# First jobs of a layer-1 attention between the tiles of the down projection, in buffers of their own

## The chip, the core and the metric

The kernel runs on one core of one Trainium2 chip. Its time is the device time of one launch in microseconds (us). The core's engines work side by side and wait for each other only through semaphores: PE (TensorE, matmuls and transposes into PSUM), DVE (VectorE), ACT (ScalarE), POOL (GpSimd), and SP, which issues most of the loads.

## The reference

Two decoder layers over x of 4 x 256 tokens and 256 channels. Each layer adds to x an attention, a state-space model (SSM) with a gate, and a feed-forward part. The stretch that is changed is the end of layer 0's feed-forward part, layer 1's attention, and beside both the steps of layer 1's SSM, which depend on the context alone:

```python
x = x + _L0_ffn_ref(_layernorm(x), ...)      # hdn = silu(g) * u ; out = hdn @ down_w
x = x + _L1_attn_ref(_layernorm(x), ...)     # 16 heads, 4 key heads, D = 128, causal
x = x + _L1_xattn_ref(ctx_1024, _layernorm(x), ...)

qkv = x @ w_qkv                              # q, k: layernorm over D, then rotary
q = q * cos + _rotate_half(q) * sin
weights = softmax(q k^T / sqrt(D), causal)
attn = weights @ v ; out = attn @ w_o

def step(state, xs):                         # the SSM: a scan over 256 tokens,
    dA = exp(d_t[..., None] * A)             # for 16 states of 256 channels
    state = state * dA + (d_t * u_t)[..., None] * B_t
    y_t = einsum('ben,bn->be', state, C_t)
```

## The kernel before

All engines run hand-written programs; the order on each is the order of the code, and every engine is in order. Tokens lie on partitions in 8 tiles of 128 (two per batch element b = 0 to 3).

**Feed-forward of layer 0.** The up projection runs over 12 half tiles j (PE L1631, ACT L730, DVE L1216 and L1219). The down projection (PE L1651, function `fd`) makes 8 output tiles of 12 matmuls each into PSUM banks 4 and 5 (tokens of b = 0, 1, "half 0") and 2 and 3 (half 1). DVE then adds a half to x (`fd_residual`, L1053), takes its layernorm statistics (L1024, L1028), POOL makes the reciprocal root (L393, L394), DVE applies it (`ln_apply`, L1033), PE transposes the half (`ln_tr`, L1474), and ACT and DVE copy it to hT (L622, L1039).

**Quarter steps.** Layer 1's SSM has 64 of them (4 batch elements x 16 states). A step q is: ACT, two exponentials into dA (L605); DVE, the product (`dbq`, L997) and the scan (`scanq`, L1006); POOL, the product with C (L403); PE, 4 transposes that accumulate (`accq`, L1435). The buffers form a ring of 8. The first `Q_IN_FFN` steps stand in code of the feed-forward part, the others in the attention's plan.

**Attention 1.** Per batch element there is a job for the keys (i = 0), four for the queries (i = 1 to 4), each for 512 columns, and one for the values. A job (b, i): PE projects (L1671, 8 matmul passes); ACT squares (`sq`, L757); DVE multiplies with the rotary tables (`rot`, L1257, L1261), sums the squares (`sum`, L1269); POOL makes the reciprocal root (L459, L460); DVE adds and scales (`rope`, L1274, 8 x L1280); PE transposes (`tr`, L1708) and ACT copies (`trc`, L768). The tables come from `tables()` (L1203 to L1207, 10 DVE instructions). A unit u = 0 to 63 is one head of one b: PE the scores (`s`, L1718 the mask by a matmul with the identity, L1719, L1720), DVE two maxima (`max`, L1288, L1289), ACT two exponentials (`exp`, L782, L784), DVE the division (`norm`, L1294, L1296, L1297), PE three transposes (`pt`, L1729), ACT a copy (`ptc`, L791), PE the values (`pv`, L1738, L1739), ACT a copy (`at`, L797), PE the output projection (`o`, L1750).

**What sets the order.** The function `att1_plan` writes one list, `ATT1_PLAN`; each engine walks it and takes its own kinds. In slot u stand, in this order, `s` of u + 1, a job's `tr`, `norm` of u - 1, `pv` of u - 2, `max` and `exp` of u, `o` of u - 3, `proj` and `acc`, `da`, `sq`, `pt` of u - 1, then `rope`, `rot`, `sum` and the quarter steps. Jobs are put in by hand at slots relative to units; the quarter steps are dealt out by `att1_plan` from the costs of the jobs and PE's load. `bank_order` says which PE work has to have left banks 0 and 1 before a projection or a transpose may write there (`BEFORE`). ACT takes the square of job j only when DVE has summed job j - 1 (L755).

Of the kernel before, what the change touches and what calls it, by code (L numbers as in the profile page):

```python
# [2061 lines left out]
```

## Time and profile before

| | us |
|---|---|
| three runs, median | 913.36 (910.98 to 916.4) |
| the profiled execution | 913.75 |
| its span | 912.0 |
| DVE busy | 703.3 (77%) |
| PE busy | 767.7 (84%) |
| ACT busy, POOL busy | 445.6 (49%), 340.6 (37%) |

The span runs from the first to the last instruction of the profile; the profiled execution is 1.75 us longer than it. The share of an engine is over all stages. Attention 1 lies between about 334 and 674 us of the span.

### The profile page before, as it was taken

What the parts mean: (1) busy time and instruction counts of PE and PEld (TensorE: products, weight loads), DVE (VectorE), ACT (ScalarE), POOL (GpSimd) and SP (SyncE); (2) the same over time, 40 slices, a digit from 0 to 9 for tenths busy, and PEclk for the clock granted to TensorE, in tenths of its full rate; (3) what the DMA queues carried; (4) which work ended last, traced back from release to release, by engine and by line L of the source; (5) the groups of instructions that cost most, each with busy time, mean ns of one, the idle gap of its engine ahead of it and who ended that gap; (6) DMA issues with size and microseconds to landing.
All of it is one profiled execution on the core that took longest, in us unless ns stands there. A gap on an engine that the chain in (4) does not pass through costs nothing.

```text
span 912.0 us, 12288 instructions
## 1 busy us (share of the span) xinstructions
PE 767.7 (84%) x3984; PEld 563.1 (62%) x3984; DVE 703.3 (77%) x1229; ACT 445.6 (49%) x928; POOL 340.6 (37%) x242
## 2 busy tenths in 40 slices
PE   6771459877798996799999999999955799999997
PEld 2241346554433563477767776777743689999996
DVE  4869779889857976999999999999977544444443
ACT  1663368650336402666566556756642354444442
POOL 1001346552330422233333323432343286666663
PEclk9785579998799998999999999999987899999999
DMA  4313223345020212011111211111300243334431
GB/s 171 121 47 114 93 94 125 115 139 218 1 98 0 74 43 92 19 40 44 51 36 36 69 36 36 55 39 36 118 0 1 79 158 138 138 138 138 141 135 46
DMA packets 28884, 74.63 MB, mean 82 GB/s; under 512 B 3633, under 2 KB 6337, under 8 KB 28449
## 3 DMA queue, kind: packets, MB, share of 16 engines
q1 hardware_dynamic: 28384, 71.51, 23.2%
q10 hardware_dynamic: 448, 2.49, 0.8%
q8 instruction: 25, 0.41, 0.2%
q14 instruction: 27, 0.21, 0.1%
HBM read 72.55 MB, written 1.44 MB: 81 GB/s over the span
## 4 chain that ended last, share of the span: by engine, by line
PE 50%; DVE 26%; issue 11%; ACT 9%; POOL 3%; DMA 1%; POOLq 0%; DVEq 0%; SPq 0%; ACTq 0%
PE ps L1671 6%; PE ps L1785 6%; PE ps L1786 6%; PE ps L1787 6%; PE ps L1631 4%; DVE hS L976 3%; PE ps L1651 3%; PE ps L1750 3%; PE ps L1435 2%; PE ps L1738 2%; DVE arena L1280 2%; DVE hS L1006 2%; DVE ps L968 2%; PE ps L1408 1%; PE ps L1720 1%
## 5 line engine op out<-in xcount | busy, mean ns | idle before, releaser
L403 POOL TENSOR_TENSOR hS<-hS,BCb 128x512 f32<-128x512 f32 x64 | 81.6, 1278 | 131.9 <-issue 66.7
L1387 DVE SCALAR_TENSOR_TENSOR arena<-ps,arena 128x1024 f32<-128x1024 f32 x32 | 39.2, 1224 | 102.2 <-ACT arena L842 93.1
L426 POOL TENSOR_TENSOR hS<-hS,BCb 128x1024 f32<-128x1024 f32 x23 | 56.1, 2440 | 111.3 <-DVE ps L968 96.3
L1671 PE MATMUL ps<-WB,hT 128*128 128x512 f32 x192 | 88.0, 603 | 3.0 <-DVE arena L1261 2.0
L476 POOL TENSOR_TENSOR MHl<-arena,MHh 128x1024 fp32r<-128x1024 f32 x34 | 81.7, 2404 | 16.9 <-ACT MHh L845 16.9
L1416 PE MATMUL ps<-ident,hS 128*128 128x128 f32 x256 | 40.1, 311 | 54.7 <-POOL hS L426 31.2
L1785 PE MATMUL ps<-Wh,MHh 128*128 128x256 f32 x272 | 77.8, 286 | 6.0 <-POOL MHl L476 6.0
L1006 DVE TENSOR_TENSOR_SCAN hS<-dA,ps 128x512 f32<-128x512 f32 x64 | 78.1, 1220 | 2.2
L1786 PE MATMUL ps<-Wl,MHh 128*128 128x256 f32 x272 | 77.6, 285 | 0.0
L1787 PE MATMUL ps<-Wh,MHl 128*128 128x256 f32 x272 | 77.5, 285 | 0.0
L1416 PEld LDWEIGHTS ps<-ident,hS 128*128 128x128 f32 x256 | 32.6, 159 | 65.1 <-POOL hS L426 38.2
L473 POOL TENSOR_TENSOR Wl<-WB,Wh 128x512 fp32r<-128x512 f32 x34 | 47.3, 1392 | 64.2 <-ACT Wh L826 64.2
L1750 PE MATMUL ps<-WA,arena 128*128 128x256 f32 x256 | 65.7, 380 | 0.0
L1671 PEld LDWEIGHTS ps<-WB,hT 128*128 128x128 f32 x192 | 36.9, 194 | 40.6 <-issue 38.4
L976 DVE TENSOR_TENSOR_SCAN hS<-dA,ps 128x1024 f32<-128x1024 f32 x23 | 52.6, 2286 | 8.2 <-ACT dA L591 7.5
L1785 PEld LDWEIGHTS ps<-Wh,MHh 128*128 128x128 f32 x272 | 52.7, 194 | 8.3 <-POOL MHl L476 7.1
L605 ACT ACTIVATE dA<-DEL,negA 128x255 f32<-128x255 f32 x128 | 55.4, 504 | 0.0
L1785 PE MATMUL ps<-hTh,Wh 128*128 128x512 f32 x136 | 53.8, 396 | 0.0
L1786 PE MATMUL ps<-hTl,Wh 128*128 128x512 f32 x136 | 53.5, 394 | 0.0
L1786 PEld LDWEIGHTS ps<-Wl,MHh 128*128 128x128 f32 x272 | 52.8, 194 | 1.2
L1787 PE MATMUL ps<-hTh,Wl 128*128 128x512 f32 x136 | 53.1, 390 | 0.0
L1787 PEld LDWEIGHTS ps<-Wh,MHl 128*128 128x128 f32 x272 | 52.7, 194 | 0.0
(233 smaller groups left out, 1967.4 us busy)
## 6 DMA issues: line engine op xcount, KB each, us to landing
BCb<-bc_dram SPq DMA_DIRECT2D x32, 512.0 KB, 3.7
BCb<-bcq_dram SPq DMA_DIRECT2D x64, 256.0 KB, 3.1
arena<-gate_dram SPq DMA_DIRECT2D x32, 512.0 KB, 3.7
WB<-in_we SPq DMA_DIRECT2D x34, 256.0 KB, 2.7
WB<-in_wqkv SPq DMA_DIRECT2D x1, 3072.0 KB, 12.7
WA<-in_wo ACTq DMA_DIRECT2D x1, 2048.0 KB, 7.7
WA<-in_ffn SPq DMA_DIRECT2D x1, 1408.0 KB, 7.9
pkb<-in_pk SPq DMA_DIRECT2D x2, 698.0 KB, 4.7
```

The costliest lines, as they stand in the source:

```text
L403: gp.tensor_tensor(h, h, qbc(q)[:, 1:2, :].broadcast_to([P, DT, S]), ALU.mult).then_inc(s["c_ready"], 1)
L426: gp.tensor_tensor(h, h, BCb[g % SB_LOADS][:, 1:2, :].broadcast_to([P, DT, HALF]), ALU.mult).then_inc(s["c_ready"], 1)
L476: gp.tensor_tensor(MHl[:, p, :], MH[p], MHh[:, p, :].bitcast(F32), ALU.subtract).then_inc(s["m_lo"], 1)
L605: sc.activation(qring(dA, q)[:, d, 1:S], DEL[:, d, S * b + 1:S * b + S], ACT.Exp, scale=negA[:, d * DS + n:d * DS + n + 1]).then_inc(s["da ...
L976: v.tensor_tensor_scan(f(h), f(a), f(dbu(g)), 0.0, ALU.mult, ALU.add).then_inc(s["scan_done"], 1)
L1006: v.tensor_tensor_scan(f(qring(hS, q)), f(qring(dA, q)), ps[:, DBQ_BANK, :], 0.0, ALU.mult, ALU.add).then_inc(s["scan_done"], 1)
L1416: last = mm(ps[:, ACC_BANK + j // 2, 256 * (j % 2) + P * d:256 * (j % 2) + P * d + P], src[:, d, P * j:P * j + P], ident[:], start=(first ...
L1671: last = mm(ps[:, bank + t, :], hT[:, c, P * (2 * b + t):P * (2 * b + t) + P], WB[:, c, c0:c0 + 512], start=(c == 0), stop=(c == HC - 1))
L1750: last = mm(ps[:, 5, 256 * t:256 * t + 256], aT1[u % 2][:, P * t:P * t + P], WO1[:, h, :], start=(h == 0 and t == 0), stop=(h == H1 - 1), ...
L1785: mm(out, wh, xh, start=start, stop=False, **kw)
L1786: mm(out, wh, xl, start=False, stop=False, **kw)
L1787: return mm(out, wl, xh, start=False, stop=stop, **kw)
```

## The change

- `Q_IN_FFN` goes from 10 to 14, so steps 10 to 13 stand ahead of the attention's plan.
- `tables()` moves from behind the first half's layernorm into the up projection, behind half tile 3.
- The down projection's tiles 4, 5 come first, then the transposes of half 0, tile 6, the projections of jobs 0 and 1, and only then tile 7 and the transposes of the quarter steps.
- Jobs 0 and 1 get buffers of their own (free arena, pkb, H, ctxp), job 1 banks 4 and 5, the values of b = 0 banks 2 and 3.
- The residual of half 1 stands between the two jobs' `rot` and `sum`; its statistics go to slot 4, its `ln_apply` to slot 6, its transposes to slot 11.
- Jobs (0, 2), (0, 3), (0, 4) go to slots -1, 2 and 4 (they were at -3, 0 and 3).
- The mask matmul writes 256 columns in place of 384.

```diff
-Q_IN_FFN = 10
-Q_GROUP_ENDS = (1, 3, 7, 9, QSTEPS - 1)
+Q_IN_FFN = 14
+Q_GROUP_ENDS = (1, 7, 8, 9, 13, QSTEPS - 1)
...
-        job_bank = lambda j: 2 if j == 1 else 0
...
-        v_bank = lambda b: 0 if b else 4
+        tok2 = lambda a: a.rearrange("p (t n) -> p t n", t=2)
+        JA_FIRST = [tok2(ar(24, 1024)), tok2(pkb[:, 0:1024])]
+        JB_FIRST = [tok2(ar(28, 1024)), tok2(H[:, 0:4, :].rearrange("p a b -> p (a b)"))]
+        JS_FIRST = [tok2(ar(36, 1024)), tok2(ctxp.rearrange("p b s -> p (b s)")[:, 0:1024])]
+
+        job_bank = lambda j: 4 if j == 1 else 0
...
+        v_bank = lambda b: 0 if b else 2
...
+                if j == 3:
+                    tables()
...
-            quarters(step, 2)
+            quarters(step, 1)
             ln_apply(3, 0)
-            tables()
-            fd_residual(1)
-            ln_stats(3, 1)
+            quarters(step, 1)
             ln_tr_copy(2, 0)
-            ln_apply(3, 1)
+            quarters(step, 4)
...
-            fd(0)
+            fd(0, 1, 2, 3)
             for k in range(4):
                 accq(next(step))
-            fd(1)
-            for q in step:
-                accq(q)
+            fd(4, 5)
             ln_tr(2, (0,))
+            fd(6)
...
-                mm(ps[:, 2 + p, 0:3 * P], identb[:], mask1[:], start=True, stop=True, skip_group_check=True)
+                diagonal = lambda z: z.rearrange("p (k n) -> p k n", k=3)[:, 0::2, :]
+                mm(diagonal(ps[:, 2 + p, 0:3 * P]), identb[:], diagonal(mask1[:]), start=True, stop=True, skip_group_check=True)
...
-    rope_job(-8, 0, 0, 2, 3)
-    rope_job(-7, 0, 1, 2, 3)
-    at(-7, "wo1", 0)
-    at(-6, "ln1", 0)
-    v_job(-5, 0)
+    first, second = (0, 0), (0, 1)
+    both = lambda j: [(kind, j + (x,)) for x in range(2) for kind in ("tr", "trc")]
+    ramp = [("proj", first), ("sq", first), ("proj", second), ("sq", second), ("fd7", 0),
+            ("rot", first), ("sum", first), ("rot", second), ("fd1", 0), ("sum", second),
+            ("v", 0), ("vc", 0), ("wo1", 0), ("rope", first)] + both(first) + [("rope", second)] + both(second)
+    rope_job(-1, 0, 2, 2, 3)
+    rope_job(2, 0, 3, 2, 4)
+    rope_job(4, 0, 4)
+    at(4, "stats1", 0)
+    at(6, "apply1", 0)
+    at(11, "ln1", 0)
...
-    plan = []
+    plan = ramp
```

PE from the first four tiles of the down projection to the first scores, before (L1651 the down projection, L1474 the layernorm's transposes, L1671 projections, L1708 a job's transposes, L1718 to L1720 scores):

```order
L1651 MATMUL ps<-arena 128x256 x24
L1435 MATMUL ps<-ident,hS 128x128 x16
L1651 MATMUL ps<-arena 128x256 x24
L1435 MATMUL ps<-ident,hS 128x128 x16
L1474 MATMUL ps<-ident,H 128x128 x8
L1671 MATMUL ps<-WB,hT 128x512 x8
L1474 MATMUL ps<-ident,H 128x128 x8
L1708 MATMUL ps<-ident,arena 128x128 x8
L1671 MATMUL ps<-WB,hT 128x512 x4
L1708 MATMUL ps<-ident,arena 128x128 x8
L1671 MATMUL ps<-WB,hT 128x512 x4
L1718 MATMUL ps<-mask,identb 128x384
```

The same place of the changed kernel (L1663, L1486, L1682, L1719 and L1732 are the same functions):

```order
L1663 MATMUL ps<-arena 128x256 x24
L1447 MATMUL ps<-ident,hS 128x128 x16
L1663 MATMUL ps<-arena 128x256 x12
L1486 MATMUL ps<-ident,H 128x128 x8
L1663 MATMUL ps<-arena 128x256 x6
L1682 MATMUL ps<-WB,hT 128x512 x8
L1663 MATMUL ps<-arena 128x256 x6
L1447 MATMUL ps<-ident,hS 128x128 x32
L1682 MATMUL ps<-WB,hT 128x512 x4
L1719 MATMUL ps<-ident,arena 128x128 x8
L1719 MATMUL ps<-ident,pkb 128x128 x8
L1732 MATMUL ps<-mask,identb 128x2x128
```

The two projections now stand ahead of the last down-projection tile, and the third job's projection, which stood ahead of the first scores, stands behind them. Half 1's transposes have left this place.

DVE of the changed kernel from the second job's `sum` (L1275) to the first steps of the plan, slots 0 to 2 (L1280 and L1286 `rope`, L1294 and L1295 `max`, L1263 and L1267 `rot`, L1300 `norm`, L1003 and L1012 a step):

```order
L1275 TENSOR_REDUCE jst<-ctxp 128x8
L1280 TENSOR_TENSOR arena<-arena 128x1024
L1286 SCALAR_TENSOR_TENSOR arena<-arena,jst,tabs 128x128 x8
L1280 TENSOR_TENSOR pkb<-pkb,H 128x1024
L1286 SCALAR_TENSOR_TENSOR pkb<-pkb,jst,tabs 128x128 x8
L1294 TENSOR_REDUCE nm<-ps 128x1
L1295 TENSOR_REDUCE nm<-ps 128x1
L1263 TENSOR_TENSOR arena<-ps,tabs 128x1024
L1267 TENSOR_TENSOR arena<-ps,tabs 128x8x64 x2
L1275 TENSOR_REDUCE jst<-arena 128x8
L1300 RECIPROCAL rc<-sum 128x2
```

Before, DVE's rows at that place, from the third job's `rot` on:

```order
L1257 TENSOR_TENSOR arena<-ps,tabs 128x1024
L1261 TENSOR_TENSOR arena<-ps,tabs 128x8x64 x2
L1269 TENSOR_REDUCE jst<-arena 128x8
L1288 TENSOR_REDUCE nm<-ps 128x1
L1289 TENSOR_REDUCE nm<-ps 128x1
L1274 TENSOR_TENSOR arena<-arena 128x1024
L1280 SCALAR_TENSOR_TENSOR arena<-arena,jst,tabs 128x128 x8
L997 TENSOR_TENSOR ps<-DU,BCb 128x512
L1006 SCALAR_TENSOR_TENSOR hS<-dA,ps 128x512
L1294 RECIPROCAL rc<-sum 128x2
```

The third job's `rot` and `sum` stood ahead of the first `max` and a quarter step ahead of the first `norm`; now they stand between that `max` and `norm`, and no step.

ACT of the changed kernel in slots 0 to 2 (L774 `trc`, L763 `sq`, L788 and L790 `exp`, L797 `ptc`, L803 `at`, L611 the exponentials of steps 14 to 18):

```order
L774 COPY arena<-ps 128x512 x4
L763 ACTIVATE arena<-ps 128x1024
L788 ACTIVATE arena,sum<-ps,nm 128x128
L790 ACTIVATE arena,sum<-ps,nm 128x256
L788 ACTIVATE arena,sum<-ps,nm 128x128
L790 ACTIVATE arena,sum<-ps,nm 128x256
L797 COPY arena<-ps 128x384
L774 COPY arena<-ps 128x512 x2
L803 COPY arena<-ps 128x256
L788 ACTIVATE arena,sum<-ps,nm 128x128
L790 ACTIVATE arena,sum<-ps,nm 128x256
L611 ACTIVATE dA<-DEL,negA 128x255 x10
```

Before, the ten exponentials stood behind the first `exp`; now they stand behind the third. The dealt-out steps per slot, from 0 to 16, were 1 0 1 1 0 1 1 0 1 1 0 1 1 3 0 1 1 and are 0 0 2 0 0 0 3 0 0 0 0 1 1 3 0 0 1; slot 47 had one and has none, and otherwise the slots from 17 to 52 hold the same as before. Slots 7 to 10 hold `rope` of (0, 4) with `rot` and `sum` of (1, 0); nothing; `proj` of (1, 1) with `rope` of (1, 0); `rot` and `sum` of (1, 1).

## Rows read from the trace of the kernel before

**Rows 1.** Windows: busy us and count of PE, PEld, DVE, ACT, POOL; PEclk; DMA.

```profile
334.00:378.00 44.00, 30.17 (x99) 17.01 (x99) 31.99 (x68) 15.42 (x34) 9.35 (x10) 0.88 0.13 48
378.00:668.00 290.00, 278.66 (x1487) 209.28 (x1488) 281.64 (x632) 177.42 (x526) 98.83 (x87) 1.00 0.16 48
```

**Rows 2.** DVE in time: start, us, line, tiles, count, idle before with its releaser.

```profile
276.70 0.69 DVE L1216 SCALAR_TENSOR_TENSOR arena<-arena,ps 128x512 f32<-128x512 f32 x1 [7.48 <-ACT arena L730]
...
320.41 0.67 DVE L997 TENSOR_TENSOR ps<-DU,BCb 128x512 f32<-128x512 f32 x1
...
324.31 2.31 DVE L1033 TENSOR_SCALAR H<-X,lnmv,lnrs 128x256 f32<-128x256 f32 x4
...
326.54 0.41 DVE L1203 TENSOR_TENSOR tabs<-arena 128x256 f32<-128x256 f32 x1
...
329.80 0.42 DVE L1207 TENSOR_TENSOR tabs<-tabs,arena 128x256 f32<-128x256 f32 x1
...
331.25 1.22 DVE L1053 TENSOR_TENSOR X<-X,ps 128x1024 f32<-128x1024 f32 x1 [1.03 <-PE ps L1651]
...
335.66 1.39 DVE L1033 TENSOR_SCALAR H<-X,lnmv,lnrs 128x256 f32<-128x256 f32 x4 [0.90 <-POOL lnrs L394]
...
361.82 1.22 DVE L1257 TENSOR_TENSOR arena<-ps,tabs 128x1024 f32<-128x1024 f32 x1 [5.68 <-ACT arena L757]
...
365.28 0.28 DVE L1288 TENSOR_REDUCE nm<-ps 128x1 f32<-128x128 f32 x1
```

**Rows 3.** PE in order of time, down projection and attention.

```profile
319.25 11.89 PE L1651 MATMUL ps<-arena 128*128 128x256 f32 x48
...
357.12 3.60 PE L1671 MATMUL ps<-WB,hT 128*128 128x512 f32 x8
...
372.22 0.55 PE L1729 MATMUL ps<-ident,arena 128*128 128x128 f32 x3 [3.35 <-DVE arena L1297]
...
390.03 1.04 PE L1708 MATMUL ps<-ident,arena 128*128 128x128 f32 x8
...
403.25 0.33 PE L1718 MATMUL ps<-mask,identb 128*128 128x384 bf16 x1
...
406.46 0.49 PE L1729 MATMUL ps<-ident,arena 128*128 128x128 f32 x3
```

**Rows 4.** Windows of 2 us, for the granted clock (PEclk).

```profile
374.00:376.00 2.00, 2.00 (x9) 1.66 (x9) 2.00 (x3) 0.01 (x1) 0.00 (x0) 0.50 0.00 0
...
378.00:380.00 2.00, 1.46 (x8) 0.91 (x8) 1.97 (x5) 2.00 (x8) 1.53 (x2) 1.00 0.00 0
```

**Rows 5.** DVE in order of time, units 6 to 9 and the norm of unit 12.

```profile
399.67 0.14 DVE L1294 RECIPROCAL rc<-sum 128x2 f32<-128x2 f32 x1
...
400.84 1.21 DVE L1257 TENSOR_TENSOR arena<-ps,tabs 128x1024 f32<-128x1024 f32 x1
...
404.29 0.15 DVE L1294 RECIPROCAL rc<-sum 128x2 f32<-128x2 f32 x1
...
408.56 1.21 DVE L1274 TENSOR_TENSOR arena<-arena 128x1024 f32<-128x1024 f32 x1
...
411.91 0.69 DVE L997 TENSOR_TENSOR ps<-DU,BCb 128x512 f32<-128x512 f32 x1
...
413.77 0.14 DVE L1294 RECIPROCAL rc<-sum 128x2 f32<-128x2 f32 x1
...
427.88 0.14 DVE L1294 RECIPROCAL rc<-sum 128x2 f32<-128x2 f32 x1
```

**Rows 6.** DVE in order of time, near the attention's end.

```profile
644.61 0.17 DVE L1294 RECIPROCAL rc<-sum 128x2 f32<-128x2 f32 x1 [1.00 <-ACT arena L784]
```

**Rows 7.** ACT in order of time, attention 1.

```profile
366.73 4.08 ACT L605 ACTIVATE dA<-DEL,negA 128x255 f32<-128x255 f32 x10
...
390.67 1.08 ACT L768 COPY arena<-ps 128x512 f32<-128x512 f32 x2 [0.78 <-PE ps L1708]
```

**Rows 8.** POOL in order of time, up projection.

```profile
264.35 8.88 POOL L445 TENSOR_TENSOR WB<-WB,wmean 128x2560 f32<-128x2560 f32 x2 [16.73 <-DVE wmean L1194]
```

More of the change, by code:

```diff
@@ L289, in build @@
         TR_LNS = [0, 2, 3, 5]
-        TR_BANK = [(4, 6), (0, 2), (0, 4), (0, 2)]
+        TR_BANK = [(4, 6), (0, 2), (0, 0), (0, 2)]
         CONV_BANK = [0, 4]
@@ L452, in _ @@
                 times_cq(q)
-            ln_rstd(3, (1,))
             def job(j):
@@ L464, in _ @@
                     job(JOB[a])
+                elif kind == "stats1":
+                    ln_rstd(3, (1,))
                 elif kind == "dbu" and a > Q_IN_FFN:
@@ L1301, in _ @@
                     job(*a)
+                elif kind == "fd1":
+                    fd_residual(1)
+                elif kind == "stats1":
+                    ln_stats(3, 1)
+                elif kind == "apply1":
+                    ln_apply(3, 1)
                 elif kind == "ln1":
@@ L1645, in _, with fd @@
             pe.wait_ge(s["wdn_ready"], NI)
-            def fd(hf):
-                for t in range(4 * hf, 4 * hf + 4):
+            def fd(*tiles):
+                for t in tiles:
                     for i in range(NI):
                         m = mlen(i)
-                        last = mm(ps[:, FD_BANK[hf] + (t % 4) // 2, 256 * (t % 2):256 * (t % 2) + 256], hid0[0:m, i, P * t:P * t + P], WDN[0:m, i, :],
+                        last = mm(ps[:, FD_BANK[t // 4] + (t % 4) // 2, 256 * (t % 2):256 * (t % 2) + 256], hid0[0:m, i, P * t:P * t + P], WDN[0:m, i, :],
                                   start=(i == 0), stop=(i == NI - 1))
@@ L1684, in banks_free @@
                     pe.wait_ge(s["job_tr_copied"], 2 * JOB[b[:2]] + 2)
+                elif was == "ln1":
+                    ln_ready(2, 1)
                 else:
@@ L1689, in v_job @@
                 if b == 0:
-                    ln_ready(2, 1)
+                    pe.wait_ge(s["x_new"], XN_FFN)
                 banks_free("v", b)
@@ L1714, in s1 @@
                 pe.wait_ge(s["job_tr_copied"], 2 * max(JOB[b, 0], JOB[b, 1 + g]) + 2)
+                if u == 0:
+                    pe.wait_ge(s["v_copied"], 1)
                 if u >= 2:
@@ L1756, in _ @@
                     v_job(a)
+                elif kind == "fd7":
+                    fd(7)
+                    for q in step:
+                        accq(q)
                 elif kind == "ln1":
+                    banks_free("ln1", 0)
                     ln_tr(2, (1,))
@@ L1892, in v_job @@
         at(slot, "vc", b)
-    rope_job(-8, 0, 0, 2, 3)
-    rope_job(-7, 0, 1, 2, 3)
-    at(-7, "wo1", 0)
-    at(-6, "ln1", 0)
-    v_job(-5, 0)
+    first, second = (0, 0), (0, 1)
[9 more added lines that the diff above has]
+    at(11, "ln1", 0)
     for b in range(B):
         u = H1 * b
-        rope_job(u - 3, b, 2)
-        rope_job(u, b, 3)
-        rope_job(u + 3, b, 4)
+        if b:
+            rope_job(u - 3, b, 2)
+            rope_job(u, b, 3)
+            rope_job(u + 3, b, 4)
         if b + 1 < B:
@@ L1950, in att1_plan @@
             plan += [("pt", u - 1), ("ptc", u - 1)]
-        plan += pick("wo1", "rope", "rot", "sum")
+        plan += pick("rope", "rot", "sum", "stats1", "apply1")
         for kind, m in now:
@@ L1969, in bank_order @@
 def bank_order():
-    claims = [p for p in ATT1_PLAN if p[0] in ("proj", "v") or (p[0] == "tr" and p[1][2] == 0)]
-    claims = [p for p in claims if p != ("v", 0) and (p[0] == "v" or p[1][:2] != (0, 1))]
+    claims = [p for p in ATT1_PLAN if p[0] in ("proj", "v", "ln1") or (p[0] == "tr" and p[1][2] == 0)]
+    claims = [p for p in claims if p != ("v", 0) and (p[0] in ("v", "ln1") or p[1][:2] != (0, 1))]
     before = {}
```

10 lines of the change are left out of this document (3 added, 7 removed).

## The prediction

> **What bounds it now.** I read the windows first, since the page's shares are means over all stages: 77% for DVE and 84% for PE say nothing of one stage. In the steady part of attention 1 DVE is busy 281.6 of 290 us and PE 278.7 [rows 1]: the two are nearly tied, DVE a little ahead. In the ramp before it (44 us) DVE is busy 32.0 and PE 30.2, so DVE idles 12.0 us there [rows 1]. DVE in order of time shows where: it waits 5.68 us for the square of the third job, after which the first maximum comes at 365.28 [rows 2]. In the steady part I followed DVE from one `norm` to the norm three units later: 399.67 to 413.77, 14.10 us, made of three times norm and maxima (1.17), a `rot` with `sum` (3.45), a `rope` (3.35) and two steps of 1.86 each [rows 5]: 3.5 + 3.45 + 3.35 + 3.7 = 14.0. So DVE's own work fills the period. What counts is how much earlier DVE begins it, and how much of that lead new waits eat.
>
> **The tables: -3.7.** Ten DVE instructions, 326.54 to 330.2 [rows 2], go into the up projection. There DVE has 7.48 us of idle time ahead of 276.70, ended by ACT [rows 2], from 269.2 on: 3.7 us fit. Cover is ACT's half tile; without it the cost would be the same 3.7 (bounds 0 and 3.7, I take 0, as the idle time is twice as long). POOL's two products of 128x2560 run there, from 264.35 to 273.23 [rows 8]. No row shows a DVE instruction with two inputs from SBUF meeting such a POOL instruction and being stopped; the nearest is the same `ln_apply` at 2.31 us and at 1.39 us [rows 2]. Were the first table product to begin only at 273.23, the tables would end at 276.9, 0.2 us behind 276.70.
>
> The Trainium skill (SBUF — State Buffer, section "Who interferes with whom") speaks against this move: a DVE instruction with two SBUF inputs contends with a GpSimd instruction that reads SBUF, and whoever issues first blocks the other. By it the sum would be 0.2 us longer, by the rows 0; no run so far tells.
>
> **The ramp: first maximum 11.4 us earlier.** I add up DVE of the changed order from the product of step 8 at 320.4. A step there is half of 320.41 to 324.31, 1.95 us [rows 2]. Step 8 to 322.4; half 0's apply (2.31) to 324.7; step 9 to 326.6; the copy to hT to 327.3 (that copy and half 1's statistics together are 2.3 us: 332.5 to 334.8, between the residual's end and the idle time ahead of 335.66 [rows 2]; I split them 0.7 and 1.6); steps 10 to 13, 7.8 us, to 335.1; `rot` and `sum` of job 0 (3.45) to 338.5. PE isn't late: four tiles take 11.89 us, 2.97 each [rows 3], tiles 4 and 5 end at 325.2, the transposes and tile 6 at about 329, the two projections (3.60 with the clock at full [rows 3], so 3.5 each) at 336, tile 7 at 339. But ACT may square job 1 only after the sum of job 0: from the start of a projection to `rot` are 361.82 - 357.12 = 4.70 us [rows 2, 3], 1.2 of them behind the projection, and DVE idles those 1.2, to 339.7. `rot`, `sum` and the residual (1.25 [rows 2]) end at 344.4, two `rope` (6.7 by [rows 5]) at 351.1. Transposes to copies are 390.03 to 391.75, 1.7 us [rows 3, 7]; mask and scores I estimate at 1.0, three times the mask's 0.33 [rows 3]. The first maximum comes at 353.8 to 353.9, against 365.28.
>
> DVE has by then done four more steps (+7.8), but not the third job's `rot` and `sum` (3.45) nor half 1's statistics (1.6), apply (1.4) and hT copy (0.7). **The lead is 11.4 + 7.8 - 7.15 = 12.0 us of DVE's work.** Every other item of the plan is the same in number, so the end comes earlier by the lead less the new idle time.
>
> **How the lead is spent: -10.8.**
> - 4.0: the third job's projection now stands behind the first scores on PE. They end at 353.7; with the 4.70 above `rot` can start at 358.4, while DVE is free at 354.4. Late behind it are that job's `sum`, and the `norm` of unit 0, for these stand behind `rot` on DVE.
> - 2.0: steps 14 and 15 stand in slot 2. Their scans need ACT's exponentials, 0.41 each, ten in 4.08 us [rows 7], and ACT reaches these after unit 2's at about 366.3; DVE is there at 368.4, they are done at 370.4. No step stands there to cover.
> - 1.0: slot 8 holds nothing between maxima and norm. The same place near the end shows a 1.00 us wait for ACT [rows 6].
> - 2.2: `rot` of (1, 1). Its projection stands on PE behind the scores of unit 10, which wait for unit 8's exponentials (1.0), then PE's own 3.2 us between a mask and the next transposes [rows 3] and the 4.70: 8.9 us, against 6.7 of DVE work.
> - 1.6: the hT copy in slot 11 waits for half 1's transposes, which PE takes late in that slot.
>
> These five are my estimates from the rows; each could be 0, if buffers let PE run ahead, and each could be half as large again. The `norm` after unit 12 would stand at about 430.6; before it stood at 427.88 [rows 5] with two steps (3.9) less done: 1.2 us are left of the lead.
>
> **Emptied slots: +2.1.** Slots 15 and 47 lose a step each. DVE then waits for the exponentials as above, so each slot saves 0.9 and not 1.95. 2 x 1.05 = 2.1. Up to here the net is -1.2 + 2.1 = **+0.9**.
>
> **PE's clock: +1.8.** Before, PE idled 3.35 us ahead of 372.22, and the granted clock was 0.50 (1.2 GHz) in 374 to 376 and 1.00 (2.4 GHz) in 378 to 380 [rows 3, 4]. In the changed kernel slot 7 holds a `rope` and a `rot` with `sum` (6.8 us) with no step between: PE has finished by 403.15 and waits for the `norm` until 407.3, 4.15 us, more than those 3.35. A fall as before, over 372.2 to 378 at most, costs PE half of 5.8, 2.9 us. DVE has 1.17 us of norm and maxima to go on with [rows 5], so 1.8. Bounds are 0 and 2.9.
>
> **Mask matmul: 0.** A third of 0.33 us [rows 3] times 64 is 7.0 us of PE and none of DVE. With DVE as the bound it gives nothing; the part of DVE's 8.4 us of steady idle time [rows 1] that is a wait for PE could shrink, so the bounds are 0 and -7.0, nearer to 0 because most of that idle time is for exponentials.
>
> **Sum** against the profiled execution, 913.75 (0.4 above the median 913.36): 913.75 + 0.9 + 1.8 = 916.5. The small differences of apply (2.31 or 1.39) and the wait for the reciprocal root (0.90 [rows 2]) add 1.5 to either side.
>
> **Rivals.**
> - *No fall of the clock* (0.20): speaks for it that the fall before followed a ramp in which PE idled 13.8 of 44 us [rows 1], while here PE works almost without a gap ahead of the 4.15. 916.5 - 1.8 = 914.7.
> - *The lead is kept* (0.27), the other side. If the scans, the norm of unit 8, the second group's projection and the hT copy find their inputs ready, only the 4.0 and the 2.1 are lost: -12.0 + 4.0 + 2.1 = -5.9, 907.9. For it: PE's work per three units is below DVE's 14.1, so PE may have a lead in slots 4 to 12 that my chain underrates, and the narrower mask adds to it. It decides once less than 4.9 us of waits follow the lead (12.0 - 2.1 - 5.0, the last to get from 913.75 to 908.8). Against it: in the slots without a step a wait of DVE for ACT shows already, 1.00 [rows 6].
> - *The clock falls in the ramp too* (0.18): PE idles from 346.7 to 353 while DVE does `rope`, and the projection of the third job then runs at half rate: 3.5 us more, straight on DVE's wait. 916.5 + 3.5 = 920.0.
> - *It doesn't do what it says*: the first maximum doesn't come earlier, because PE reaches projections as late as before. Its two tiles and the transposes' places speak against that; I give it no chance of its own. What I call forecast (0.35) is +2.7.
>
> **How the numbers follow.** Some 0.5% (4.6 us) is what measuring this kernel can tell from no change: below 908.8 and above 917.9. The forecast's own range is 914 to 919 (clock 0 to 2.9, 1.5 of small items). Faster: most of the kept lead, 0.25. Slower: the 0.18 and the upper part of the forecast, 0.28. Same: 0.47. Of the kept lead the part below 907 and of the ramp's clock the part above 920.5 stay outside, 2 in 10.
>
> **What would show it.** Right: the tables in front of the row at 276.70 with its idle time cut to 3.8; the first maximum near 354; 4.0 us idle before the third `rot`; a wait of 2 us for ACT before step 14's scan; 1.0 before the norm of unit 8; about 2 before `rot` of (1, 1) and 1.6 before the hT copy; a window with clock 0.50 near 408; and 14.1 us for three units later on, as before. Wrong: those idle times near 0 and the norm of unit 12 before 428 (kept lead); clock 0.50 between 350 and 362 (the ramp's); a steady period below 14.0 (the mask counts, PE was the bound).

## The result, and the profile after

| | before | changed |
|---|---|---|
| median of 8 runs, us | 913.38 (910.98 to 916.4) | 921.92 (919.77 to 923.52) |
| profiled execution, us | 913.75 | 923.52 |
| span, us | 912.0 | 921.7 |
| first maximum, us | 365.28 | 355.36 |
| `norm` of unit 12, us | 427.88 | 438.57 |
| `norm` of unit 63, us | 667.61 | 678.83 |

The ratio is 1.0083, with a 95% interval of 1.0064 to 1.0103: slower by 0.8%, outside the forecast's range. The first maximum came 9.9 us earlier. From there to unit 12's `norm` the changed kernel lost all of that and 10.7 us more. The profiled execution of the changed kernel is the slowest of its eight, 1.6 us above their median.

The windows of the changed kernel for the stretches of [rows 1] (busy us and count of PE, PEld, DVE, ACT, POOL; PEclk; DMA):

```profile
334.00:378.00 44.00, 33.57 (x132) 20.61 (x130) 29.28 (x58) 13.04 (x32) 9.51 (x9) 0.84 0.19 68
378.00:668.00 290.00, 269.52 (x1409) 199.45 (x1410) 270.13 (x618) 170.37 (x498) 91.52 (x81) 0.98 0.14 45
```

In the first 44 us DVE has 14.7 us idle (44 - 29.28), where [rows 1] have 12.0, though it starts with more steps done. In the steady stretch it has 19.9 us idle where there were 8.4, and PE 20.5 where there were 11.3: both engines wait more than before.

DVE of the changed kernel in order of time, from the tables on (the value in brackets is the idle time ahead of the row and what ended it):

```profile
269.09 4.38 DVE L1209 TENSOR_TENSOR tabs<-arena 128x256 f32<-128x256 f32 x1
...
276.76 0.69 DVE L1222 SCALAR_TENSOR_TENSOR arena<-arena,ps 128x512 f32<-128x512 f32 x1
...
326.95 1.41 DVE L1003 TENSOR_TENSOR ps<-DU,BCb 128x512 f32<-128x512 f32 x1
...
340.38 1.22 DVE L1263 TENSOR_TENSOR pkb<-ps,tabs 128x1024 f32<-128x1024 f32 x1 [1.15 <-ACT ctxp L763]
...
355.36 0.29 DVE L1294 TENSOR_REDUCE nm<-ps 128x1 f32<-128x128 f32 x1 [3.59 <-PE ps L1734]
...
362.02 1.23 DVE L1263 TENSOR_TENSOR arena<-ps,tabs 128x1024 f32<-128x1024 f32 x1 [6.04 <-ACT arena L763]
...
375.49 1.22 DVE L1012 TENSOR_TENSOR_SCAN hS<-dA,ps 128x512 f32<-128x512 f32 x1 [3.58 <-issue]
...
413.17 0.17 DVE L1300 RECIPROCAL rc<-sum 128x2 f32<-128x2 f32 x1 [0.98 <-ACT arena L790]
...
418.35 0.17 DVE L1300 RECIPROCAL rc<-sum 128x2 f32<-128x2 f32 x1 [0.54 <-ACT arena L790]
...
422.80 1.23 DVE L1263 TENSOR_TENSOR arena<-ps,tabs 128x1024 f32<-128x1024 f32 x1 [3.17 <-ACT arena L763]
...
429.71 0.69 DVE L1045 COPY hT<-ps 128x512 f32<-128x512 f32 x1 [2.18 <-PE ps L1486]
...
452.59 0.17 DVE L1300 RECIPROCAL rc<-sum 128x2 f32<-128x2 f32 x1 [0.98 <-ACT arena L790]
...
526.90 1.23 DVE L1263 TENSOR_TENSOR arena<-ps,tabs 128x1024 f32<-128x1024 f32 x1 [2.52 <-ACT arena L763]
...
535.33 0.17 DVE L1300 RECIPROCAL rc<-sum 128x2 f32<-128x2 f32 x1 [1.83 <-ACT arena L790]
...
613.05 0.17 DVE L1300 RECIPROCAL rc<-sum 128x2 f32<-128x2 f32 x1 [1.28 <-ACT arena L790]
```

Read beside [rows 2]: the tables end ahead of 276.76, where 276.70 stood. Each wait that the prediction named is there, but larger: 6.04 us ahead of the third `rot` (4.0 forecast), 3.58 ahead of step 14's scan (2.0), 0.98 and 0.54 (1.0), 3.17 ahead of `rot` of (1, 1) (2.2), 2.18 ahead of the hT copy (1.6). The rows at 452.59 and 613.05 are the emptied slots 15 and 47 (1.05 each forecast). Those at 526.90 and 535.33 were not forecast.

The row at 375.49 names no releaser ("issue"). ACT's row shows it: the ten exponentials begin at 374.50, forecast for 366.3, and the scan follows behind the first two of them.

```profile
374.50 4.08 ACT L611 ACTIVATE dA<-DEL,negA 128x255 f32<-128x255 f32 x10
```

PE of the changed kernel, same columns, from the second job's transposes to the third projection:

```profile
351.82 1.13 PE L1719 MATMUL ps<-ident,pkb 128*128 128x128 f32 x8 [2.27 <-DVE pkb L1286]
...
353.64 0.40 PE L1732 MATMUL ps<-mask,identb 128*128 128x256 bf16 x1 [0.69 <-ACT arena L774]
...
355.11 5.82 PE L1682 MATMUL ps<-WB,hT 128*128 128x512 f32 x8
...
366.28 0.83 PE L1741 MATMUL ps<-ident,arena 128*128 128x128 f32 x3 [2.41 <-DVE arena L1303]
...
370.17 1.97 PE L1719 MATMUL ps<-ident,arena 128*128 128x128 f32 x8 [0.66 <-DVE arena L1286]
```

And its granted clock, in windows of 2 us (the number after the five engines):

```profile
350.00:352.00 2.00, 0.18 (x2) 0.18 (x3) 1.77 (x7) 0.23 (x1) 0.00 (x0) 1.00 0.85 360
354.00:356.00 2.00, 2.00 (x7) 1.30 (x6) 0.62 (x2) 0.00 (x0) 0.00 (x0) 0.50 0.27 115
362.00:364.00 2.00, 0.93 (x5) 0.55 (x5) 1.98 (x3) 0.80 (x4) 0.00 (x0) 1.00 0.00 0
368.00:370.00 2.00, 1.51 (x5) 0.78 (x4) 2.00 (x8) 0.07 (x1) 0.00 (x0) 0.50 0.00 0
414.00:416.00 2.00, 2.00 (x10) 1.89 (x9) 1.97 (x5) 0.74 (x2) 0.00 (x0) 0.55 0.00 0
```

The projection takes 5.82 us where [rows 3] has 3.60. The clock is at 0.50 (1.2 GHz) from about 353 to 359, after PE had waited 2.27 us for the second `rope` and 0.69 for a copy, and again from about 367 to 373, behind a wait of 2.41: the third job's transposes at 370.17 take 1.97 us, where [rows 3] has 1.04 for such a row. At 414 it is 0.55, behind waits of PE of 1.77 and 1.02 us; the single gap of 4.15 us that was forecast there isn't in the trace. The rival "the clock falls in the ramp too" (920.0) had the fall right, and it stood at 0.18; the measured 921.9 is above its sum as well. The kernel before has a fall in its ramp too, 0.50 from 346 to 352 behind 4.69 us of PE's idle time, which the prediction did not look at.

### The profile page after: what moved, and what is told of

It is laid out like the page before. It is cut to its first block, busy times and chain, and to the rows that moved or that the text cites. A ratio compares the mean times of both kernels' runs of the same rounds, so it can differ in the third digit from the quotient of the medians.

```text
span 921.7 us, 12288 instructions
## 1 busy us (share of the span) xinstructions
PE 771.4 (84%) x3984; PEld 563.6 (61%) x3984; DVE 708.2 (77%) x1229; ACT 446.6 (48%) x928; POOL 340.9 (37%) x242
## 4 chain that ended last, share of the span: by engine, by line
PE 40%; DVE 36%; issue 11%; ACT 10%; POOL 2%; DMA 1%; POOLq 0%; DVEq 0%; SPq 0%; ACTq 0%
PE ps L1802 6%; PE ps L1803 6%; PE ps L1804 6%; DVE hS L1012 5%; PE ps L1643 4%; PE ps L1682 3%; DVE arena L1286 3%; DVE hS L982 3%; DVE ps L1003 3%; ACT dA L611 2%; DVE jst L1275 2%; DVE arena L1267 2%; PE ps L1762 2%; DVE ps L974 2%; PE ps L1750 2%
## 5 line engine op out<-in xcount | busy, mean ns | idle before, releaser
L1682 PE MATMUL ps<-WB,hT 128*128 128x512 f32 x192 | 88.6, 606 | 1.5 <-DVE X L1059 1.5
L1012 DVE TENSOR_TENSOR_SCAN hS<-dA,ps 128x512 f32<-128x512 f32 x64 | 78.1, 1220 | 5.7 <-issue 3.6
L1762 PE MATMUL ps<-WA,arena 128*128 128x256 f32 x256 | 67.7, 389 | 0.0
L1682 PEld LDWEIGHTS ps<-WB,hT 128*128 128x128 f32 x192 | 37.3, 196 | 39.6 <-issue 36.6
L611 ACT ACTIVATE dA<-DEL,negA 128x255 f32<-128x255 f32 x128 | 55.2, 503 | 0.9 <-DVE hS L1012 0.9
L1750 PE MATMUL ps<-arena 128*128 128x256 f32 x128 | 44.3, 429 | 12.6 <-ACT arena L797 11.0
```

Source lines behind the costliest of these rows:

```text
L611: sc.activation(qring(dA, q)[:, d, 1:S], DEL[:, d, S * b + 1:S * b + S], ACT.Exp, scale=negA[:, d * DS + n:d * DS + n + 1]).then_inc(s["da ...
L1012: v.tensor_tensor_scan(f(qring(hS, q)), f(qring(dA, q)), ps[:, DBQ_BANK, :], 0.0, ALU.mult, ALU.add).then_inc(s["scan_done"], 1)
L1682: last = mm(ps[:, bank + t, :], hT[:, c, P * (2 * b + t):P * (2 * b + t) + P], WB[:, c, c0:c0 + 512], start=(c == 0), stop=(c == HC - 1))
L1750: mm(ps[:, 4, 0:S], va[:, 0, D1 * g:D1 * g + D1], PT1[u % 2][:, 0:S], start=True, stop=True, skip_group_check=True)
L1762: last = mm(ps[:, 5, 256 * t:256 * t + 256], aT1[u % 2][:, P * t:P * t + P], WO1[:, h, :], start=(h == 0 and t == 0), stop=(h == H1 - 1), ...
```

## Experiments

All times are medians, beside runs of the kernel before on the same chip (913.5 to 914.0).

| run | us | ratio to before (95%) | against the changed kernel |
|---|---|---|---|
| third_in_ramp | 911.70 | 0.9978 (0.9956 to 1.0001) | -10.2 |
| steps_back | 920.33 | 1.0058 (1.0039 to 1.0077) | -1.6 |
| pe_filled | 919.72 | 1.0060 (1.0028 to 1.0091) | -2.2 |
| spread | 919.80 | 1.0068 (1.0042 to 1.0093) | -2.1 |
| mask_384 | 921.75 | 1.0096 (1.0072 to 1.0119) | -0.2 |
| ten_ahead | 930.67 | 1.0179 (1.0146 to 1.0212) | +8.8 |
| da_in_ramp | 912.17 | 0.9978 (0.9959 to 0.9998) | -9.8 |
| best1 | 905.72 | 0.9917 (0.9896 to 0.9938) | -16.2 |
| best1_filled | 904.86 | 0.9905 (0.9889 to 0.9921) | -17.1 |
| best1_ten | 912.41 | 0.9987 (0.9973 to 1.0001) | -9.5 |
| tables_only | 914.02 | 0.9994 (0.9977 to 1.0011) | |
| tables_early | 913.53 | 1.0015 (0.9987 to 1.0044) | |

The intervals are some 2 us to either side, so differences of 1.6 to 2.2 from the changed kernel are at the edge of what can be told by the medians; their traces are read beside them. spread, mask_384 and ten_ahead have four runs each.

The traces also show how far one order varies from execution to execution. steps_back, spread and mask_384 have the changed kernel's order up to the third `rot` (mask_384 but for the mask's width), but DVE waits 4.34, 4.33 and 3.87 us ahead of it, not 6.04. The scan's wait is 3.61 in all three (3.58 in the changed kernel).

### The third projection's place

```diff
+        tr_bank = lambda j: 4 if j == 0 else job_bank(j)
...
-            ("v", 0), ("vc", 0), ("wo1", 0), ("rope", first)] + both(first) + [("rope", second)] + both(second)
-    rope_job(-1, 0, 2, 2, 3)
+            ("proj", third), ("sq", third), ("v", 0), ("vc", 0), ("wo1", 0), ("rope", first)] + both(first) + [("rope", second)] + both(second) + [("rot", third), ("sum", third)]
...
```

The edit moves two things together: the third projection on PE, and on DVE the third `rot` and `sum`, which now stand ahead of the first maximum.

> The changed kernel, with the third job's projection put on PE ahead of the values' projection, the first job's transposes in banks 4 and 5, and its rot and sum on DVE behind the second rope; steps per slot as in the changed kernel. Theory (the first scores' place ahead of the third projection costs the two waits of 3.59 and 6.04 us of DVE): both go, 9.6 us less, about 912 us (ratio to the kernel before 0.999). Rival (PE is what bounds slots 0 to 11, so a lead of DVE only turns into later waits): more than half comes back as longer waits for ACT and PE in slots 1 to 12, about 917 to 919.

DVE of this kernel in order of time, at the place of 355.36 and 362.02 above, and later:

```profile
350.44 1.22 DVE L1264 TENSOR_TENSOR arena<-ps,tabs 128x1024 f32<-128x1024 f32 x1
...
353.90 0.28 DVE L1295 TENSOR_REDUCE nm<-ps 128x1 f32<-128x128 f32 x1
...
355.49 0.17 DVE L1301 RECIPROCAL rc<-sum 128x2 f32<-128x2 f32 x1 [0.98 <-ACT arena L791]
...
524.91 0.17 DVE L1301 RECIPROCAL rc<-sum 128x2 f32<-128x2 f32 x1 [3.43 <-ACT arena L791]
```

PE of the same kernel (two projections in one row, the third job's and the values'):

```profile
341.02 7.03 PE L1683 MATMUL ps<-WB,hT 128*128 128x512 f32 x16
```

Measured 911.7, as forecast to 0.3 us. The third `rot` stands at 350.44 without idle time ahead of it, the first maximum follows at 353.90, and the 9.6 us don't come back at the places near by: unit 0's `norm` waits 0.98. At 535.33's place 3.43 stand for 1.83, but that wait differs as much between executions of the changed order (below). The median is 10.2 lower. So the third job's place in the order accounts for more than the whole loss of 8.5 us. Part of this comes with the clock: the three of the ten runs whose mean clock is 0.921 or 0.922, as in the changed kernel (0.917 to 0.922), took 914.8 to 916.8, some 6.7 us under 921.9; the other seven have 0.927 to 0.931 and a median of 911.4. The trace shown is one of the three (915.22). The two projections (7.03 us together) run at full rate, ahead of the scores.

### Which slot ACT's copy of ACC stands in

```diff
-            while ssm and spent + price(ssm[0]) / 2 < total * sum(load[:u + 1]) / sum(load):
+            while ssm and spent + price(ssm[0]) / 2 < total * sum(load[:u + 1]) / sum(load) - (2.0 if 16 <= u < 47 else 0.0):
```

> The changed kernel with one quarter step moved from slot 16 to slot 47, so that every later step stands in the slot it had before the change. Theory (being one step ahead puts ACT's copy of ACC for the second batch element, which waits for PE, into the slot of rot (2, 2); there DVE waits 2.52 and 1.83 us against 0.71 before): those waits fall back to about 0.7, slot 47 gets its step back, 3.6 to 5 us less, 917 to 918 us (ratio 1.004). Rival (the late waits come from PE's clock and the ramp): no change that can be told, 921 to 922.

ACT and then PE of the changed kernel, in order of time, ahead of the wait at 526.90:

```profile
519.23 0.21 ACT L790 ACTIVATION_READ_ACCUMULATOR arena<-ps,nm 128x1 f32 x1
...
522.98 0.59 ACT L617 COPY ACC<-ps 128x512 f32<-128x512 f32 x1 [3.55 <-PE ps L1447]
```

```profile
518.91 3.60 PE L1682 MATMUL ps<-WB,hT 128*128 128x512 f32 x8
...
522.35 0.60 PE L1447 MATMUL ps<-ident,hS 128*128 128x128 f32 x4
```

ACT stands at L617, the copy of ACC once batch element 1's sixteen steps are accumulated, for 3.55 us; PE has its last accumulation (L1447) behind the projection of (2, 2). Behind the copy on ACT stand six exponentials and the square for which DVE's `rot` waits, and behind those the copy for which PE's `pv` waits. With four steps ahead and three fewer dealt, every later step came one step earlier against the slots, and this copy fell from slot 30 into slot 29, where the projection of (2, 2) stands. DVE of the run steps_back at the same units:

```profile
360.85 1.22 DVE L1263 TENSOR_TENSOR arena<-ps,tabs 128x1024 f32<-128x1024 f32 x1 [4.34 <-ACT arena L763]
...
456.87 1.23 DVE L1263 TENSOR_TENSOR arena<-ps,tabs 128x1024 f32<-128x1024 f32 x1 [1.66 <-ACT arena L763]
...
528.29 0.17 DVE L1300 RECIPROCAL rc<-sum 128x2 f32<-128x2 f32 x1 [0.66 <-ACT arena L790]
...
615.87 1.22 DVE L1263 TENSOR_TENSOR arena<-ps,tabs 128x1024 f32<-128x1024 f32 x1 [1.66 <-ACT arena L763]
```

The two waits (4.35 us) are down to 0.66, and the 1.28 at 613.05 is gone. But 1.66 us stand newly at 456.87, behind the slot that lost its step, and 1.66 at 615.87: 4.97 less and 3.32 more, and 1.6 us is what is left of the 3.6 to 5 expected; 920.33 lies between theory and rival. The cause of the first wait is shown: it is 2.50 to 2.56 us in the six traces that have the copy in slot 29, and absent in those that have it in slot 30, as here and in best1. The second wait varies in one and the same order: 0.39 in pe_filled, 1.83 in the changed kernel, 3.23 in mask_384. In all three PE idles 3.19 to 3.24 us behind the copy; behind that the clock stays at 1.00 in pe_filled and falls to 0.50 in the other two. That the alignment costs 1.6 us by itself is at the edge of the intervals.

### PE's clock

```diff
+            def fill(n):
+                for k in range(n):
+                    mm(ps[:, 4, 0:3 * P], identb[:], mask1[:], start=True, stop=True, skip_group_check=True)
...
+                if (j, x) == (1, 0):
+                    pe.wait_ge(s["job_rope"], 8)
+                    pe.wait_ge(s["job_rot"], 6)
+                    fill(13)
                 pe.wait_ge(s["job_rope"], 8 * (j + 1))
...
+                if u < 1:
+                    fill(12)
```

The 12 matmuls of unit 0 stand in front of PE's wait for its `norm`.

> The changed kernel with 13 mask matmuls of 384 columns on PE ahead of the second job's transposes and 12 ahead of unit 0's, written to bank 4 and overwritten. Theory (PE's idle stretches in the ramp drop its granted clock to 0.50, which doubles the first scores and stretches the third projection to 5.82 us): the clock stays at 1.00 in 350 to 374, the projection takes 3.6, DVE's wait of 6.04 falls to about 3.9, the one of 3.58 to about 2.5; 3 to 5 us less, 917 to 919 us. Rival (the clock falls for another reason than PE's idle time, or the fillers stand in the way): no gain, 921 to 924.

Windows of this kernel, the ramp and the steady stretch:

```profile
334.00:378.00 44.00, 34.94 (x178) 22.66 (x177) 33.64 (x69) 16.46 (x41) 9.89 (x10) 1.00 0.21 71
378.00:668.00 290.00, 269.61 (x1438) 199.43 (x1437) 273.33 (x627) 171.50 (x503) 94.11 (x82) 1.00 0.15 44
```

and PE, then DVE, at the third job:

```profile
353.05 3.60 PE L1682 MATMUL ps<-WB,hT 128*128 128x512 f32 x8
```

```profile
357.74 1.22 DVE L1263 TENSOR_TENSOR arena<-ps,tabs 128x1024 f32<-128x1024 f32 x1 [3.87 <-ACT arena L763]
...
369.73 1.22 DVE L1012 TENSOR_TENSOR_SCAN hS<-dA,ps 128x512 f32<-128x512 f32 x1 [2.11 <-issue]
```

The clock is 1.00 throughout, the projection takes 3.60, and the waits are 3.87 and 2.11 for 6.04 and 3.58, as the theory had it. The five places that the prediction named come to 11.3 us here (3.87 + 2.11 + 0.98 + 2.13 + 2.17), close to its 10.8. From the second `rot` (339.00 here, 340.38 in the changed kernel) to the `norm` of unit 63 are 330.6 us and not 338.5: this execution took 916.51. The ten runs fall into two groups: five from 914.4 to 916.9 with a mean clock of 0.930 or 0.931 over the span, and five from 922.6 to 924.4 with 0.921. So full clock goes with some 7 us in this order, but fillers at two places don't hold it in each execution, and the median of 919.72 lies between theory and rival. Nor is it shown that the fillers are what held it where it held: in the profiled execution it stays at 1.00 in the steady stretch too, where there are no fillers. In which stretch the five at 0.921 lost it is not shown, since one execution is profiled.

### Steps as cover

```diff
-            while ssm and spent + price(ssm[0]) / 2 < total * sum(load[:u + 1]) / sum(load):
+            while ssm and sum(p[0] == "step" for p in now) < STEPS_IN[u]:
```

> The changed kernel with the eleven steps of slots 0 to 16 dealt 0 0 1 0 0 1 1 0 1 1 1 1 1 2 0 0 1 in place of 0 0 2 0 0 0 3 0 0 0 0 1 1 3 0 0 1. Theory (the waits of 0.98, 0.54 and 3.17 us in slots 8 to 10 are DVE slots without a step to cover ACT's exponentials and PE's projection): they fall to 1.5 in all, 3 to 4 us less, 918 to 919 us. Rival (PE is the later engine there by its own work, and a step only fills DVE's idle time): the idle time moves to slot 6, where three steps stood, and the time stays at 920.5 to 922.

DVE of this kernel from slot 8 on:

```profile
408.54 0.14 DVE L1300 RECIPROCAL rc<-sum 128x2 f32<-128x2 f32 x1
...
418.59 1.23 DVE L1263 TENSOR_TENSOR arena<-ps,tabs 128x1024 f32<-128x1024 f32 x1 [2.38 <-ACT arena L763]
...
425.89 0.69 DVE L1045 COPY hT<-ps 128x512 f32<-128x512 f32 x1 [0.72 <-PE ps L1486]
```

The wait of 0.98 is gone and the copy waits 0.72, where the other traces of the changed order have 2.17 to 2.23; `rot` of (1, 1) still waits 2.38 for ACT's square, which a step can't hasten. The 0.54 is gone too, but it is also missing in steps_back and mask_384. New are 0.84 us ahead of the fourth `rot` (376.68), and 1.39 ahead of the `norm` at 447.61, in place of the 0.98 of slot 15. 2.1 us in all: between theory and rival, at the edge of the interval with four runs.

```diff
-Q_IN_FFN = 14
+Q_IN_FFN = 10
...
-            quarters(step, 4)
```

> The changed kernel with 10 steps ahead of the plan in place of 14; the planner deals 14 over slots 0 to 16, 0 0 2 0 1 0 2 0 0 1 0 1 1 3 0 0 2. Theory (the plan's first slots are bound by PE and by chains over PE and ACT, so steps taken out of them leave idle time on DVE and buy nothing, while they push the ramp back): the first maximum comes 2 to 5 us earlier, and slots 0 to 16 take no longer in spite of three more steps, 916 to 919 us. Rival (DVE's work is the bound, and each step ahead was done in time that was idle before): the steps come back in full, 921 to 924 us.

DVE of this kernel, first `rot` and first maximum:

```profile
332.91 1.23 DVE L1262 TENSOR_TENSOR arena<-ps,tabs 128x1024 f32<-128x1024 f32 x1 [6.62 <-ACT arena L763]
...
353.42 0.29 DVE L1293 TENSOR_REDUCE nm<-ps 128x1 f32<-128x128 f32 x1 [4.42 <-PE ps L1733]
```

My theory did not hold, and 930.67 is above the rival's 921 to 924 as well. DVE waits 6.62 us for PE's first projection and ACT's square of it, which is the time that the four steps had filled: the maximum comes only 1.9 us earlier for 7.8 us of work left over, and the whole is 8.8 us slower. (The dealing that was expected holds 13 steps in slots 0 to 16, not 14.) Why it is more than the 7.8 is not shown; the mean clock, 0.917 to 0.921 in the four runs, is that of the changed kernel.

```diff
-    ramp = [("proj", first), ("sq", first), ("proj", second), ("sq", second), ("fd7", 0),
+    ramp = [("proj", first), ("sq", first), ("proj", second), ("sq", second), ("fd7", 0)] + ssm[:6] + [
```

> The kernel with the third projection in the ramp, and the exponentials of steps 14 to 16 moved from slot 2 to the ramp on ACT; steps dealt as in the changed kernel. Theory (the scan of step 14 waits for its exponentials alone): the 3.61 us of DVE falls to 1.2 or less, 908.5 to 910 us. Rival (PE's own work in slots 2 to 6 sets the time): DVE's wait only moves to a later slot, 911 to 912 us.

The wait for the exponentials is gone in this trace, as the theory had it: from the second `rot` to unit 3's `norm` are 31.4 us and not 34.2. The medians show no gain, 912.17 and 911.70, where the rival stood. The profiled execution reached the second `rot` at 342.38, against 338.8 to 340.9 in the others with 14 steps ahead, with the same order on PE and DVE up to there. I leave open how much the 3.61 us are worth.

```diff
-                diagonal = lambda z: z.rearrange("p (k n) -> p k n", k=3)[:, 0::2, :]
-                mm(diagonal(ps[:, 2 + p, 0:3 * P]), identb[:], diagonal(mask1[:]), start=True, stop=True, skip_group_check=True)
+                mm(ps[:, 2 + p, 0:3 * P], identb[:], mask1[:], start=True, stop=True, skip_group_check=True)
```

> The changed kernel with the mask matmul over 384 columns as before. Theory (with 14 steps ahead of the plan PE is the later engine in slots 0 to 12, so its time counts there): about 0.05 to 0.1 us a unit in 20 units, 1 to 2 us more, 923 to 924. Rival (DVE is the bound throughout): no difference, 922.

No difference that can be told, 921.75: the rival, though with four runs the theory's 1 to 2 us lie within the interval. The prediction put a third of 0.33 us on the narrower mask, 7.0 us of PE in all; the matmul takes 0.27 where it took 0.33, so it is 0.06 times 64, 3.8 us.

### All together

best1 is third_in_ramp with the exponentials of da_in_ramp in the ramp, the steps of slots 0 to 16 dealt by hand, and from slot 17 on as in the kernel before. best1_filled adds fillers at three places, best1_ten has 10 steps ahead.

```diff
+STEPS_IN = [1, 0, 2, 0, 0, 1, 0, 0, 1, 1, 0, 0, 1, 2, 0, 0, 1, ...]
```

> The third job's projection in the ramp as in the run before, the exponentials of steps 14 to 16 moved from slot 2 into the ramp on ACT, and the steps dealt 1 0 2 0 0 1 0 0 1 1 0 0 1 2 0 0 1 over slots 0 to 16 and from slot 17 on as in the kernel before. Theory (each of the named waits has its own cause, and these are cured): the 3.61 of the scan goes, the 2.50 and 3.43 behind ACT's copy of ACC fall to 0.7, 911.7 - 3.5 - 4.5 = about 904 us (ratio 0.990). Rival (PE's own work bounds slots 0 to 16, and the removed waits come back there): 908 to 910 us.

> The kernel best1 with mask matmuls that are overwritten put on PE in its idle stretches ahead of the second job's transposes (5), ahead of unit 2's scores (9) and ahead of unit 0's transposes (3). Theory (PE's idle time there is what drops its clock to 0.50 from 358 on): the clock stays at 1.00 up to 378, and 1.5 to 3 us go, 903 to 904.5 us. Rival (PE's clock there is hidden behind DVE, or it falls somewhere else in its place): no difference, 905.7 us.

> The kernel best1 with 10 steps ahead of the plan and fourteen in slots 0 to 16, dealt 2 0 2 1 0 1 0 1 1 1 0 1 1 2 0 0 1. Theory (four steps ahead fill time in which DVE otherwise waits for PE's first projection, seen as 6.62 us of idle time in the run with ten ahead, and DVE pays them back slot by slot): 5 to 8 us more than best1, 911 to 914 us. Rival (the slots have room for steps, because PE is the later engine there): 905 to 908 us.

best1 took 905.72, 1.7 above the theory's 904, and is faster than both kernels: 0.83% under the one before. Two things were changed together here, the exponentials and the dealing, which also puts ACT's copy back into slot 30; the 6.0 us under third_in_ramp are not split between them. DVE of best1, the `rot` of the fourth job and the place of the ACC copy:

```profile
369.37 1.23 DVE L1264 TENSOR_TENSOR arena<-ps,tabs 128x1024 f32<-128x1024 f32 x1 [1.73 <-ACT arena L764]
...
514.70 0.17 DVE L1301 RECIPROCAL rc<-sum 128x2 f32<-128x2 f32 x1 [0.66 <-ACT arena L791]
```

The fillers moved the first fall of the clock from 358 to 360 and changed nothing that can be told (904.86, the intervals overlap). Ten steps ahead cost 6.7 us here (912.41, within the theory's 911 to 914), with the same 6.62 us of DVE idle ahead of the first `rot`. Four steps ahead are worth about their 7.8 us in either order, 6.7 and 8.8. The wait of the hT copy behind half 1's transposes is 2.28 us in best1: no run moved those transposes, and what their place costs stays open. The buffers and banks were not tested by themselves either.

### The tables and POOL

```diff
+                if j == 3:
+                    tables()
...
             ln_apply(3, 0)
-            tables()
```

> The kernel before with the rotary tables in the up projection behind half tile 3 and nothing else. Theory (DVE's first table product is held by POOL's product until 273.2, 4 us, and fits all the same): the tables end at about 276.8, DVE has 3.7 us more room ahead of half 1's residual, which then waits for PE until 331.25 as before; since that residual waited for PE, only part comes through, 0 to 2 us less, ratio 0.998 to 1.000. Rival (all of DVE's ramp work is on the path): 3.7 us less, ratio 0.996.

> The kernel before with the tables behind half tile 2 of the up projection, where DVE is idle for 1.96 us and POOL is in the first of its two products of 128x2560. Theory (a DVE product with both inputs in SBUF waits until the POOL product ahead of it is over): the first table product takes some 3 us, to POOL's end of the first at 268.8, and half tile 3's products start about 4.5 us late at 272; PE's gap is less, since the next half tile on DVE was idle 7.48 us. Rival (the 4.38 us seen behind half tile 3 had another cause, as the first use of rope tables' data): 0.41 us here, or 4.38 again.

(tables_early has `j == 2`.) POOL, then DVE of tables_early:

```profile
264.15 9.07 POOL L445 TENSOR_TENSOR WB<-WB,wmean 128x2560 f32<-128x2560 f32 x2 [16.72 <-DVE wmean L1194]
```

```profile
265.51 3.38 DVE L1203 TENSOR_TENSOR tabs<-arena 128x256 f32<-128x256 f32 x1
...
268.82 4.68 DVE L1204 TENSOR_TENSOR tabs<-arena 128x256 f32<-128x256 f32 x1
...
276.46 0.69 DVE L1216 SCALAR_TENSOR_TENSOR arena<-arena,ps 128x512 f32<-128x512 f32 x1
```

Two table products in a row, which take 0.41 us alone, take 3.38 and 4.68 us: the first ends as POOL's first product of 128x2560 does (halfway between 264.15 and 273.2, at 268.7), the second as POOL's second does. The theory had only the first of them held. Behind half tile 3 one product took 4.38 us. The tables end at 276.4 in any case, and the time is that of before. tables_only (914.02, before 913.59) gains nothing either: on DVE half 1's residual then waits 4.56 us for PE in place of 1.03 ([rows 2]), 3.5 of the 3.7.

```profile
330.26 1.22 DVE L1053 TENSOR_TENSOR X<-X,ps 128x1024 f32<-128x1024 f32 x1 [4.56 <-PE ps L1652]
```

## Why the prediction was wrong

- **Tables: -3.7.** Right in place and end (276.7), and the rule of the Trainium skill (SBUF — State Buffer, "Who interferes with whom") is what the trace shows: 4.38 us for a product of 0.41. It cost nothing here, since DVE's idle time covered it. But the 3.7 us are worth something only if DVE has work to put in their place; alone they gave nothing that can be told.
- **The ramp: first maximum at 353.9.** 355.36, with the profiled execution some 0.7 us late there already (second `rot` at 340.38, forecast 339.7). The rest is PE, with the scores at half clock: DVE waits 3.59 us ahead of the maximum, and 2.85 in pe_filled. The step's mechanism was right, 1.5 us too good.
- **"How the lead is spent: -10.8".** This step failed, by size. The five places and their releasers were all right; in the profiled execution they measured 6.04 + 3.58 + 1.52 + 3.17 + 2.18 = 16.5 us, 5.7 more. I had priced the projection at 3.6 and the chains over PE at full clock, and had put the fall of the clock only behind slot 7. At full clock (pe_filled) the five come to 11.3, so it is PE's clock that was priced wrong. How much it takes depends on the execution: 16.5 in the profiled one, 13.2 in steps_back, 12.9 in mask_384.
- **A term was missing, in "Emptied slots: +2.1".** The waits in slots 15 and 47 are as forecast (0.98 and 1.28, forecast 1.05 each). But the step looked at single slots and not at what the shift moves: ACT's copy of ACC met a projection in slot 29, 4.35 us of waits for 0.71 before. Here too the rest is the clock: 2.9 us in pe_filled, 5.8 in mask_384.
- **Clock: +1.8.** The fall in slots 8 and 9 came (0.55 at 414), though the 4.15 us gap that was to cause it did not. It is in the 3.17 and 0.54: pe_filled has 2.13 and nothing there, 1.6 us less. In steps_back the clock falls earlier (0.62 and 0.53 in 404 to 408), ahead of slot 8's `norm`, and the wait is 2.12 with nothing beside it: there it cost nothing. That 1.8 fits the profiled execution is partly luck. Of the 5.7 above this step had already paid 1.8.
- **Mask: 0.** Right as far as can be told, with PE's saving put at 7.0 us and measured at 3.8.
- In sum, read from the traces: at the first maximum 9.9 us earlier, at unit 12's `norm` 10.7 later (forecast 2.7). Of these 20.6 us DVE is idle for 16.6 (17.9 for 1.3) and busy for 4.0 (65.3 for 61.3): the third job's and half 1's work that stood ahead of the first maximum before, less two steps. From unit 12 to unit 63 it is +0.5: 4.5 more idle, most of it the copy and the emptied slots, and 4.0 less busy, again two steps fewer. Behind the attention 1.5 come back, 1.1 of it where DVE waits 8.0 for the gate's load and not 9.1; this is no effect of the order, as that stretch took 242.9 us here and 244.4 to 246.5 in the kernel before, steps_back, mask_384, pe_filled and third_in_ramp. That is +9.7 on the span.

What I had not asked: whether the third projection must stand behind the first scores. PE's order, not DVE's load, held the two largest waits.

## What to carry to other kernels

When a change gives one engine a lead, list in order what each other engine has in its queue at that point: the lead lasts only as far as their next item is early too, and one projection in the wrong place on PE took 10.2 us by the medians, where everything else together moved 6. Work dealt out by a planner's running sum moves everything behind it when a few items leave the front; look for the copies and waits that are bound to a count of steps, not to a slot. Price a chain over PE at both levels of its clock if PE idles ahead of it. And before a wait is explained by its size in one trace, look for it in the traces of other runs that share the order up to there: the largest wait here was 6.04 us in one execution and 3.9 to 4.3 in three others.
